# A four-layer graph network stack: the second norm's scale and shift on ScalarE, VectorE left with its shift alone, and a new order of steps

## The reference, cut to what matters

```python
def reference(x, adj, nodemask, ...):              # x, adj: 128 graphs, each 128 x 128, float32
    x = layernorm(x + L0(x, adj))     # GCN on five small groups of nodes, fused
    x = layernorm(x + L1(x, adj))     # attention: 8 heads of 16, scores + log(adj + 1e-6), output product
    x = layernorm(x + L2(x, adj))     # relu(norm_adj @ (x W + b))
    x = layernorm(x + L3(x, adj))     # five gated (GRU) layers over A = (adj != 0)
    return x

def layernorm(x):                     # over the last axis, no gain and no bias
    m, v = mean(x), var(x)
    return (x - m) / sqrt(v + 1e-5)
```

## Time and profile before

| | us |
|---|---|
| median of 3 runs | 1725.01 (1722.77 to 1726.6) |
| the profiled execution's own time | 1734.59 |
| its span, first to last instruction | 1732.8 |

### The profile page before, as it was taken

One profiled execution on the slowest core, in us unless ns is written; L12 is line 12 of the kernel. 1 busy time (PEld: TensorE's weight loads), 2 busy tenths in 40 slices (PEclk: granted clock), 3 DMA queues, 4 the chain that ended last, 5 costly groups with the idle time before them and its releaser, 6 DMA issues.

```text
span 1732.8 us, 33734 instructions
## 1 busy us (share of the span) xinstructions
PE 1630.8 (94%) x12076; PEld 1337.4 (77%) x12076; DVE 1365.1 (79%) x3531; ACT 1315.7 (76%) x3122; POOL 781.2 (45%) x843
## 2 busy tenths in 40 slices
PE   6779999999999999999999999999999999999984
PEld 5567788787878878787887878788787878777763
DVE  4577897878789787878978787897878789787753
ACT  1367788787778878777887878788787878888663
POOL 2133454535445453544545354444535444453432
PEclk9799999999999999999999999999999999999997
DMA  3000100101010010101001010100001010000000
GB/s 91 20 23 19 30 13 26 29 13 29 25 29 14 26 29 14 29 26 29 14 26 28 14 29 26 29 14 27 28 13 29 26 29 14 26 13 14 13 6 12
DMA packets 84800, 40.93 MB, mean 24 GB/s; under 512 B 10629, under 2 KB 84634, under 8 KB 84634
## 3 DMA queue, kind: packets, MB, share of 16 engines
q1 hardware_dynamic: 84058, 38.62, 8.1%
q10 hardware_dynamic: 576, 0.15, 0.0%
HBM read 30.36 MB, written 8.39 MB: 22 GB/s over the span
## 4 chain that ended last, share of the span: by engine, by line
PE 79%; DVE 11%; ACT 7%; issue 2%; POOL 1%; DMA 0%; POOLq 0%; DVEq 0%; SPq 0%; ACTq 0%
PE RA L931 17%; PE RB L931 16%; PE Q L885 8%; PE RT L1111 8%; PE RT L885 4%; PE Q L1036 4%; ACT x L513 3%; PE M L885 3%; PE Q L1051 3%; PE M L973 2%; PE M L966 2%; PE Q L1017 2%; PE M L1079 2%; DVE stats L643 2%; PE Q L1021 2%
## 5 line engine op out<-in xcount | busy, mean ns | idle before, releaser
L496 POOL TENSOR_TENSOR h_lo<-hT,h_hi 128x512 fp32r<-128x512 f32 x160 | 210.3, 1314 | 548.4 <-ACT h_hi L592 520.1
L570 ACT ACTIVATE e_s<-Q,s_ng 128x128 f32<-128x128 f32 x1024 | 297.8, 403 | 19.2 <-DVE s_ng L750 17.1
L499 POOL TENSOR_TENSOR hd<-hT,nn 128x512 f32<-128x512 f32 x160 | 206.5, 1291 | 36.2 <-ACT nn L604 36.1
L598 ACT ACTIVATE tr<-RA,b_rz 128x512 f32<-128x512 f32 x160 | 114.7, 717 | 101.5 <-PE RA L931 101.5
L604 ACT ACTIVATE nn<-tr,wT 128x512 f32<-128x512 f32 x160 | 117.4, 734 | 96.2 <-DVE tr L804 96.2
L756 DVE TENSOR_TENSOR p_s<-Q,adjTe 128x512 f32<-128x512 f32 x256 | 172.1, 683 | 21.3 <-PE Q L885 21.1
L750 DVE TENSOR_REDUCE s_ng<-Q 128x4 f32<-128x512 f32 x256 | 167.8, 681 | 9.7 <-PE Q L1036 8.5
L800 DVE SCALAR_TENSOR_TENSOR un<-tr,un 128x512 f32<-128x512 f32 x160 | 109.8, 686 | 75.1 <-ACT un L601 75.1
L796 DVE TENSOR_TENSOR agg_lo<-RT,agg_hi 128x512 fp32r<-128x512 f32 x160 | 110.0, 688 | 71.6 <-ACT agg_hi L595 69.5
L885 PE MATMUL Q<-ident,e_s 128*128 128x128 f32 x1024 | 156.5, 276 | 9.7 <-ACT e_s L570 9.6
L885 PEld LDWEIGHTS Q<-ident,e_s 128*128 128x128 f32 x1024 | 125.4, 142 | 34.5 <-ACT e_s L570 14.2
(11 more groups left out here) (194 smaller groups left out, 4362.6 us busy)
## 6 DMA issues: line engine op xcount, KB each, us to landing
adjn<-in_adj_dram SPq DMA_DIRECT2D x32, 256.0 KB, 2.9
xin<-in_x_dram SPq DMA_DIRECT2D x32, 256.0 KB, 3.4
adjr<-in_adj_dram SPq DMA_DIRECT2D x32, 256.0 KB, 3.1
out_dram<-x SPq DMA_DIRECT2D x32, 256.0 KB, 2.4
adjc<-in_adj_dram SPq DMA_DIRECT2D x124, 4.0 KB, 2.2
xs<-in_x_dram SPq DMA_DIRECT2D x120, 16.0 KB, 1.8
W1s<-in_L_gnn_W_dram SPq DMA_DIRECT2D x1, 640.0 KB, 4.9
W2s<-in_L_gnn_W_dram SPq DMA_DIRECT2D x2, 320.0 KB, 4.8
```

The costliest lines, as they stand in the source:

```text
L496: pool.tensor_tensor(h_lo[g][:, :], hT[g][:, :], h_hi[g][:, :], ALU.subtract).then_inc(SG["h_lo"][g], 1)
L499: pool.tensor_tensor(hd[g][:, :], hT[g][:, :], nn[g][:, :], ALU.subtract).then_inc(SG["hd"][g], 1)
L570: ins = act.activation(e_s[:, j, c, :], Q[j][:, c * P:(c + 1) * P], ACT.Exp, bias=s_ng[:, j, c:c + 1])
L598: act.activation(tr[g][:, :], RA[:, :], ACT.Tanh, bias=b_rz[:, 0:1], scale=0.5).then_inc(SG["r_act"][g], 1)
```

## The change

The second norm's scale and shift move to ScalarE. VectorE keeps one small instruction, which forms the shift nm2; ScalarE gets a step `x2` that waits for it and applies both in four ACTIVATE instructions. A tile `nm2` and a semaphore are added. To keep the number of semaphores, `zeros_ready` is merged into `consts_ready`: who waited for the one now waits for the third count of the other. All eight strings of `MERGE` are replaced, and ScalarE's now place a step there that had been empty on that engine.

```diff
 MERGE = dict(
-    scalar=("AARABRRRARBBARARRRAAAAAARRBRRBRBRBRBRRBRRRABBBAAARARARBRARRARARARARRRRARRAARBRAARBAARBRARABRAAARRABARRRR",
+    scalar=("AARBABRRRBARBARARRRAAABAARRARRARARBRABRRRRRRRARABARBBBRRRABRBABRRRARRAARARARRAARBARARARBABRRARAAAABRRABRRRRA",
...
+        nm2 = [sb(f"nm2_{g}", [P, GB]) for g in range(NG)]
...
-            pool.memset(vp[0][:, :, :, DH:DH + 1], 1.0).then_inc(zeros_ready, 1)
+            pool.memset(vp[0][:, :, :, DH:DH + 1], 1.0).then_inc(consts_ready, 1)
...
+                elif kind == "x2":
+                    wait(act, "nm2", it, g + 1)
+                    normalise(x2[g], y2[g], rs[g][1], nm2[g]).then_inc(S["x2"], 1)
...
                 elif kind == "x2":
                     wait(dve, "ln2_pow", it, g + 1)
-                    normalise(x2[g], y2[g], mv[g][1], rs[g][1]).then_inc(S["x2"], 1)
+                    shift(nm2[g], mv[g][1], rs[g][1]).then_inc(S["nm2"], 1)
                     wait(dve, "deg_pow", it, g + 1)
```

More of the change, by code:

```diff
@@ L34 @@
     o_mm=1, o_relu=1, fused=2, fused_mm=NG, y1=NG,
-    ln1=2 * GB * NG, ln1_eps=NG, ln1_pow=NG, ln2=2 * GB * NG, ln2_eps=NG, ln2_pow=NG, ln3=2 * GB * NG, ln3_eps=NG, ln3_pow=NG, x1=NG, x2=NG,
+    ln1=2 * GB * NG, ln1_eps=NG, ln1_pow=NG, ln2=2 * GB * NG, ln2_eps=NG, ln2_pow=NG, ln3=2 * GB * NG, ln3_eps=NG, ln3_pow=NG, x1=NG, x2=NG, nm2=NG,
     adjt_mm=NG, adj_t=NG, adj_te=NG, x1t_mm=NG, x1_t=NG, x1_b=NG, k_mm=NG, q_mm=NG, v_mm=NG, k_t=2 * NG, q_t=NG, v_p=NG,
@@ L51 @@
 MERGE = dict(
[L52 to L55, removed]
-    scalar=("AARABRRRARBBARARRRAAAAAARRBRRBRBRBRBRRBRRRABBBAAARARARBRARRARARARARRRRARRAARBRAARBAARBRARABRAAARRABARRRR",
-            "AARRAARRRRBRARRARRRARARAAARRRABAARRRBABARBARBARBRARAARRABAAARRRARBRBRRRARRRARRAARRARARABRAAARRARR"),
-    gpsimd=("ARBRRRBAARRBRAARRARAARAAARRBRRRARARBARRBRRABAAABRAARABARRRARRARBAARARABRRRRBARRRRRARBBRBBBBAARAARAAARRRR",
-            "AARRRBAAARRARRRRRRAARRRRRRRAARRBARRBBAARARRABRAARRBRRBRAAARRRRRBBAABRRRARRAABRAAAAAAARRRRAAARRRAA"),
+    tensor=("BAARBRARRBRAARABRAARRRRARRBRAARABRRAARABBRRBABRRARBRARBABBRRRRRRBAARRAARRARABARRARRAARRARARBAAARAABRRARR",
+            "AABRARRBRRRARRAARRRRAARAAARRBAARRBRAARARARBRRBAARABRRARBAAAARRARARRARBARRBRRRRRARRAARAAARRARRRRBA"),
+    vector=("RRBBAABRARRAARABAARAAARRRARRARRRABBRARRRRARBBBBARARBRBRAARBRRARRBARABARBRAAARARRRARRARRRRRBAAAARRARRRABA",
+            "RAABRRARRARARRAARARBRARAARRRARAAABRRRAAABRRRBARRBAABAAAARRARRRARBBRRRAARARRBRRRRRRRARRARAAABARRAR"),
+    scalar=("AARBABRRRBARARRAAABAARRARRARARBRABRRRRRRRARABARBBBRRRABRBABRRRARRAARARARRAARBARARARBABRRARAAAABRRABRRRRA",
+            "AABRARARRBRRRARRARAAARRARRARARABAARRBARRRABRBBRAAARRRRAAAABARRRARRBRRBARRARRAARRRAAARRAARRABRRRAR"),
+    gpsimd=("RBRRARRARRBBRRBRAAARRAAAARARRARRRAAAABARBAAARARARRBBBRABRRBAARARRRRBRARRRRBAABBRARRRRRRRRAABBAAARARRARAB",
+            "BAARRARRRRRBRRRRRRRRRRRAARAAARAAAARBARRAAAAABARAABABRARBAAARRRBAAARARARRRRAARBABRRRBAARRRRRRRRARR"),
 )
@@ L142, in gnn_stack_kernel @@
         w_exp, w_pool = sem("w_exp"), sem("w_pool")
-        zeros_ready, fw_in, bias_in, first_in, w_fuse = (sem(n) for n in ("zeros_ready", "fw_in", "bias_in", "first_in", "w_fuse"))
+        fw_in, bias_in, first_in, w_fuse = (sem(n) for n in ("fw_in", "bias_in", "first_in", "w_fuse"))
         w_first, w_comp = sem("w_first"), sem("w_comp")
@@ L536, in steps @@
                     if it == 0:
-                        act.wait_ge(zeros_ready, 1)
+                        act.wait_ge(consts_ready, 3)
                     wait(act, "z_mm", it, 1)
@@ L871, in _ @@
             after(dve.tensor_scalar(wT[:, WQ, :], wT[:, WQ, :], SCALE, None, ALU.mult))
-            dve.wait_ge(zeros_ready, 1)
+            dve.wait_ge(consts_ready, 3)
             for kind in ("adj_t", "l0_fuse", "l0_add"):
```

## The result

In the same session the kernel before took 1723.72 us (median of 13 runs) and the changed one 1729.74 (13 runs): a ratio of 1.0034, 95% interval 1.0022 to 1.0045. The change makes it slower by 6 us. One of the changed kernel's 13 executions took 1857.48 us at a mean granted clock of 0.841, and the ratio leaves it out. The profiled execution took 1728.59 us, its span is 1726.8. The two spans differ by 3.7 us and not by 6.0: the trace of the change is of its fastest execution, 1.15 us under its median, and that of before is of one that took 1725.02 us, 1.3 above the median of 1723.72.

A forecast was written before the change was run, and what follows sets the result against it. TensorE's matmuls were taken as the bound, busy 98.70 of 100.83 us per iteration. Terms of 4.2 us (steady), 1.3 (tail) and 0.7 (head) sum to 6.2 us slower, giving 1731 us; range 1716 to 1740.

The forecast's parts named there:

- signs of being wrong: Steady iteration under 100.8 us with smaller seam waits and earlier y in half 1, or no TensorE wait outside the seam.
- the seam: Passage from half 1 to half 0, holding all TensorE's steady waits, 2.0 us per iteration; its gain was put at nothing.
- the first rival: Half 1's y starts earlier, so the seam shortens by up to 0.68 us per iteration: 1717.5 us; chance 0.27.
- Half 0, +0.15 through a_r: x2 ahead of tr on ScalarE delays a_r, so adj transposes start some 0.15 us late; bounds 0 and 0.26.
- The slack is 0.14 us, and TensorE asks no later than before: Half 0: a_r ended at 934.41, the adj transposes that must wait for it started at 934.55.
- Half 1, +0.15: x2 between tz and o_ts on ScalarE makes the second pair's exponentials late: 0.15 us on TensorE, bounds 0 and 0.57.
- VectorE's relief comes where it buys nothing: The 0.96 us VectorE saves in half 1 lie ahead of gaps where it waits for ScalarE and TensorE anyway.
- Steady sum: Steady iterations: 14 times 0.15 us for half 0 plus 0.15 for half 1, 4.2 us slower.
- The tail, 1.3: After the last rs, nm2 and x2 on ScalarE delay x2's transposes and tr: 1.3 us, bounds 0.7 and 1.8.
- The head, 0.7: VectorE does nat and the first norm ahead of the second pair's third maximum: 0.7 us, bounds 0 and 1.7.
- 1.7 us of delay, of which the products in between hide most: Head: nat (0.59 us) and first norm (1.12) delay the third maximum; products cover all but 0.7 us.
- The lock: GpSimd's hd beside nm2 blocks their shared port, x2 starts 1.07 us later: up to 1742 us; chance 0.08.

The follow-up runs named there:

- e3: The changed kernel's new order, with the second norm's scale and shift (x2) kept on VectorE; 1735.14 us, ratio 1.0055 to the kernel before.
- e6: The changed kernel, but half 0 in the old order with x2 on VectorE; half 1 new with x2 on ScalarE; 1727.25 us, ratio 1.001 to before.
- e9: The kernel before's order, with only group 1's x2 on ScalarE, placed early ahead of tr, and nm2 earlier on VectorE; 1733.57 us, ratio 1.0035 to before.
- e14: Old half 0 with x2 on VectorE, new half 1 with x2 on ScalarE, plus 127 transposes filling TensorE's head waits; 1719.58 us, ratio 0.9957 to before.
- e7: The changed kernel, with nat and x1 moved behind h_new on VectorE in half 0, and TensorE's sel product later; 1733.56 us, ratio 1.0048 to before.
- e12: The changed kernel, with the sixth exponentials' transposes ahead of the turn of layer 2 on TensorE in half 0; 1739.94 us, ratio 1.0068 to before.
- e10: The changed kernel, with 134 small transposes filling TensorE's waits in the head; 1725.53 us, ratio 0.9992 to the kernel before.
- e11: The kernel before, with the transposes that filled the changed kernel's head waits put in the same places; 1726.17 us, ratio 0.9995 to the kernel before unfilled.
- e2: The changed kernel with the kernel before's order strings, so x2 runs on ScalarE in the old order; 1785.7 us, ratio 1.0349 to before.
- e8: The changed kernel, with two TensorE steps of half 1 (l0_out and adj_t) put nearly back to their old places; 1756.42 us, ratio 1.0179 to before.

## Why the prediction was right, and where it was not

The forecast was 1731 and slower was the likeliest sign; 1729.74 came. The sum of 6.2 us was the measured 6.0, but that is luck: its terms were not the measured ones, and the traces account for 3.7 us only. One of the prediction's own signs of being wrong came true: the view of waits shows no wait of TensorE outside the seam, neither that of the adj transposes for a_r nor one of the exponentials' transposes. The iteration took 100.94 us, not 101.1.

- **The bound and the seam: right.** TensorE's matmuls take 98.73 us of an iteration. The seam's three waits are unchanged at 2.0 us, so the first rival did not come.
- **The costs of the instructions: right for the moved ones, not for the engines.** ScalarE's block is 1.65 us and its group grew by 54.9 us, predicted 53; but the engine's whole busy time grew by 37.6 us only, since in dense stretches its instructions overlap (at 873.38 tr lasts 0.76 us, and the next starts 0.57 us behind its start). VectorE lost 20.9 us, not 31. x2 and nm2 account for 30.9 less; against that nat takes 277 ns longer, 4.4 us in 16, since it now runs beside GpSimd's hd, the row maxima s_ng take 4.0 us longer, and the rest is spread.
- **Half 0, +0.15 through a_r: right sign, wrong cause.** It lost 0.33 us, but e3 loses the same with x2 on VectorE. The failed step is "The slack is 0.14 us, and TensorE asks no later than before": I let only x2 move and kept the old order around it. The adj transposes did not wait for a_r with the change. They did in e6, e9 and e14, by 0.2 to 0.3 us, with x2 on either engine, and half 0 took 51.12 us in all three: that wait costs nothing. What the change's trace shows in its place is the turn of hT, 0.27 of the 0.33 us, behind nat and GpSimd's hd (e7). Neither e7 nor e12 healed it; which of its links decides is open.
- **Half 1, +0.15: wrong sign.** It gained 0.22 us, 0.04 by the order and 0.18 by the move (e3). The failed step is "VectorE's relief comes where it buys nothing": I looked only at the seam and missed hd and hT right behind x2.
- **Steady sum: too large.** 14 x 0.30 = 4.2 was forecast. From the third to the last product it is 1.3 us.
- **The tail, 1.3: the wait right, its worth not.** The x2 transposes wait as forecast:

```profile
1615.59 1.65 ACT L514 ACTIVATE x<-y,nm,rs 128x128 f32<-128x128 f32 x4 [1.99 <-DVE nm L662]
1617.15 0.67 ACT L599 ACTIVATE tr<-RA,b_rz 128x512 f32<-128x512 f32 x1
...
1617.30 0.66 PE L890 MATMUL M<-ident,x 128*128 128x128 f32 x4 [1.23 <-ACT x L514]
```

  The lag behind before rises there from 3.5 to 4.6 us, and then falls to 3.7 at the end; from the last product on only 0.6 us remain. Why it falls again is not shown.
- **The head, 0.7: too small.** It lost 2.3 us (0.4 in its half 0, where I had looked, 1.9 in half 1). The failed step is the term of 0.7 us, "1.7 us of delay, of which the products in between hide most": it took the waits for the only price of the head and nat and the first norm for the place. The clock is another price: 1.5 of the 1.9, by e10 and e11.
- **The lock: right.** nm2 took 0.15 us in both halves (880.53 and 913.44). nm4 meets GpSimd's hd and takes 1.22 us once per iteration, before and after. The Trainium skill ("SBUF — State Buffer", SBUF: two separate sides) states the exclusive lock of the shared port; nat is a second place that agrees: at 940.01 it takes 0.91 us and ends 0.46 after GpSimd's hd (939.17 to 940.46).

## What to carry to other kernels

On engines that work in order, a step that moves to another engine costs by its place there, and by what its input waits behind: x2's 1.65 us of ScalarE cost half 0 nothing ahead of tr, with nm2 made early enough (e9), and 3.46 us behind h_hi (e2). The wait itself was only 1.87 of them; the other 1.6 were TensorE's lower clock behind it. So read the granted clock behind a new wait before the loss is put down to the wait alone, and read the starts of the matmuls too: the view of waits left out the 0.27 us at the turn of h, and 0.4 of the 0.97 us found in e8. Where a list is reordered as a whole, look first for the engines' instructions right behind and ahead of each moved step, not only at the seam that waits. Do the same for the head, and fill waits only where they are: the same fill shortened one head by 4.5 us and the other not at all.

## What was not expected of the hardware

- TensorE's clock in the head depends on what the order leaves idle. From 40 to 104 us it was 0.72 to 0.89 in stretches of 16 us in the changed kernel, and 1.00 with 134 small transposes in the waits. It can fall in the steady part too: in e2 it was 0.50 behind a wait of 1.80 us in most iterations, and stayed at 1.00 in others with the same wait; what decides between them is not shown. Runs of one kernel differ in it: e9 had two levels 8 us apart, with mean clocks of 0.985 and 0.983 (that a half-clock stretch in the head makes the upper one is argued from the first trace of before, not shown in e9).
- VectorE's nat, two inputs from SBUF, takes 0.59 us alone and 0.91 beside GpSimd's hd.
